# A source histogram kept in four quarters, with one copy per group of four tiles

## What is computed

```python
edge_index = jnp.stack([src, dst])                    # dst is sorted, src is not
msgs = jnp.exp(-edge_weight)[:, None] * x[dst]
out0 = jax.ops.segment_sum(msgs, src, num_segments=N_NODES)
seg_sum = jax.ops.segment_sum(edge_attr_32, src, num_segments=N)
seg_max = jax.ops.segment_max(edge_attr_32, src, num_segments=N)
```

## Time and profile before

| | us |
|---|---|
| median of three runs | 11958.36 |
| the profiled execution, whole | 11906.45 |
| its span, first to last instruction | 11904.7 |
| stage of the sort, first to last block's first scatter | 501.62 to 3457.44 |

### The profile page before, as it was taken

One profiled execution on the slowest core, in us unless ns is written; L12 is line 12 of the kernel. 1 busy time (PEld: TensorE's weight loads), 2 busy tenths in 40 slices (PEclk: granted clock), 3 DMA queues, 4 the chain that ended last, 5 costly groups with the idle time before them and its releaser, 6 DMA issues.

```text
span 11904.7 us, 66247 instructions
## 1 busy us (share of the span) xinstructions
PE 2340.7 (20%) x13804; PEld 1990.9 (17%) x13804; DVE 4863.0 (41%) x18501; ACT 1149.7 (10%) x3976; POOL 7239.8 (61%) x6880
## 2 busy tenths in 40 slices
PE   8755555555530041000000010000000100000000
PEld 7644444444420031000000010000000100000000
DVE  9744444444459932222222122222222444444445
ACT  0133333333320010000000000000000000000000
POOL 1555555555530035777777657777776677777776
PEclk7755555555555555555555555555555555555555
DMA  5122221222137701111111111111111122222221
GB/s 207 33 51 53 53 53 51 53 53 53 51 115 272 256 28 43 46 48 46 47 46 48 36 45 47 46 46 48 46 47 39 36 56 56 58 57 56 56 56 42
DMA packets 541753, 768.49 MB, mean 65 GB/s; under 512 B 328431, under 2 KB 341656, under 8 KB 528648
## 3 DMA queue, kind: packets, MB, share of 16 engines
q1 hardware_dynamic: 321544, 509.40, 12.8%
q0 software_dynamic: 219904, 255.88, 10.1%
HBM read 352.00 MB, written 412.82 MB: 64 GB/s over the span
## 4 chain that ended last, share of the span: by engine, by line
DVE 26%; issue 22%; POOL 20%; another core or an unknown queue 15%; PE 13%; ACT 4%; DVEq 1%; DMA 1%; SPq 0%; POOLq 0%
POOL arena_a L579 18%; DVE arena_a L1265 9%; DVE arena_a L1391 5%; PE bank L751 4%; PE bank L744 3%; DVE arena_a L1092 2%; DVE arena_a L1087 2%; PE bank L732 2%; PE bank L708 2%; PE bank L826 1%; DVE arena_a L1352 1%; ACT arena_b L663 1%; DVE arena_b L939 1%; PE bank L730 1%
## 5 line engine op out<-in xcount | busy, mean ns | idle before, releaser
L579 POOL DMA_INDIRECT arena_a<-table_c,decay x3136 | 3332.3, 1063 | 1326.1 <-issue 1002.6
L529 POOL DMA_INDIRECT by_src<-arena_b,idx_blk x1568 | 1553.0, 990 | 1500.5 <-ACT arena_b L656 1022.1
L1265 DVE SCALAR_TENSOR_TENSOR arena_a<-arena_a,same_dst 128x64 f32<-128x64 f32 x3134 | 892.3, 285 | 3447.7 <-DVE arena_a L1265 2029.0
L579 POOL DMA_INDIRECT arena_a<-table_at,decay x1568 | 1669.5, 1065 | 562.7 <-issue 474.1
L775 PE MATMUL bank<-ident,chunk_end 128*64 128x128 f32 (+2 forms) x8 | 2.7, 443 | 6672.6 <-DVEq L858 6672.6
L775 PEld LDWEIGHTS bank<-ident,chunk_end 128*64 128x64 f32 (+2 forms) x8 | 1.4, 240 | 6673.1 <-DVEq L858 6673.1
L988 DVE SCALAR_TENSOR_TENSOR arena_b<-bank,src_f,before 128x128 bf16<-128x128 f32 x1568 | 542.7, 346 | 1336.8 <-remote 1127.1
L751 PE MATMUL bank<-arena_b 98*128 98x128 f32 x3136 | 1056.4, 437 | 0.0
L744 PE MATMUL bank<-arena_b 128*98 128x128 bf16 x1568 | 526.2, 336 | 1382.7 <-ACT arena_b L663 913.5
L751 PEld LDWEIGHTS bank<-arena_b 98*128 98x128 f32 x3136 | 782.5, 306 | 0.0
L1391 DVE SCALAR_TENSOR_TENSOR arena_a<-arena_a,same_dst 128x68 f32<-128x68 f32 x1568 | 454.9, 290 | 458.6 <-DVE arena_a L1391 320.4
(11 more groups left out here) (251 smaller groups left out, 5287.3 us busy)
## 6 DMA issues: line engine op xcount, KB each, us to landing
states_src<-arena_a SPq DMA_DIRECT2D x98, 1024.0 KB
states_c<-arena_a SPq DMA_DIRECT2D x196, 512.0 KB
hrows<-by_src SPq DMA_DIRECT2D x98, 776.0 KB, 6.1
states_at<-arena_a SPq DMA_DIRECT2D x98, 576.0 KB
x_at_start<-arena_a SPq DMA_DIRECT2D x7, 7168.0 KB, 49.3
arena_a<-x_at_start SPq DMA_DIRECT2D x98, 512.0 KB, 3.7
arena_a<-table_c,decay POOLq DMA_INDIRECT x3136
arena_b<-in_a SPq DMA_DIRECT2D x98, 256.0 KB
```

The source lines that it names most:

```text
L529: pool.indirect_dma_start(out=by_src, out_offset=AT(ap=idx_blk[r][:, k:k + 1], axis=0), in_=rows[r][:, k, :], in_offset=None)\
L579: pool.indirect_dma_start(out=gb[r][:, k * w:(k + 1) * w], out_offset=None, in_=table[g], in_offset=AT(ap=src_i[:, n * J + k:n * J + k + 1 ...
L1265: ins = v.scalar_tensor_tensor(out=st[h][:, k * D:(k + 1) * D], in0=old, scalar=same_dst[:, e:e + 1], in1=gb[r][:, k * D:(k + 1) * D], op0 ...
```

## The change

`hist` becomes four histograms side by side in the same PSUM bank, one for each column modulo four, 98 x 512 in all. Quarter q of a tile's node starts at `base` plus the counts of the quarters before q. Tiles of one group no longer depend on each other, so the four tiles of a group share one copy (98x512), are added one after another, and are counted one after another. The order on each engine changes with it:

- ScalarE, for each group g: copy of the histograms for g+1, copy of the turned one-hots of g+1, then the four scalings of group g-2 (LAG is now 2, in groups). Before: 16 copies a block, and one scaling after each.
- TensorE, for each group g: four adds, twelve matmuls that turn group g+1, four counts. `hist_added` is raised once a group and no longer once a tile.
- In the bounds of the source, the histogram is counted into the four quarters; VectorE copies 98x512, sums over the quarters, and computes three further starts (98x128 each).
- `base` and the quarters live in the part of `arena_a` that is used early.

```diff
-LAG = 6
+LAG = 2
...
-        hist = bank[0][0:HIGH, 0:LOW]
+        hist = [bank[0][0:HIGH, q * LOW:(q + 1) * LOW] for q in range(Q)]
+        hist4 = bank[0][0:HIGH, 0:Q * LOW]
...
+            def snapped(g):
+                act.wait_ge(s("hist_added"), g + 1)
+                act.activation(snap[g % 2], hist4, ACT.Copy).then_inc(s("snap_ready"), 1)
+
+            snapped(0)
             turned(0)
-            for t in range(L):
-
-                act.wait_ge(s("hist_added"), t + 1)
-                act.activation(snap[t % 2], hist, ACT.Copy).then_inc(s("snap_ready"), 1)
-                if t % Q == 2 and t // Q + 1 < L // Q:
-                    turned(t // Q + 1)
-                if t >= LAG:
-                    scaled(t - LAG)
+            for g in range(L // Q):
+
+                if g + 1 < L // Q:
+                    snapped(g + 1)
+                    turned(g + 1)
+                if g >= LAG:
+                    for t in range((g - LAG) * Q, (g - LAG + 1) * Q):
+                        scaled(t)
...
-            pe.matmul(hist, ident[0:HIGH, 0:HIGH], base[:, :], start=True, stop=True).then_inc(s("hist_added"), 1)
+            pe.matmul(hist4, ident[0:HIGH, 0:HIGH], base4[:, :], start=True, stop=True).then_inc(s("hist_added"), 1)
...
+            def add(g):
+
+                pe.wait_ge(s("snap_ready"), g + 1)
+                for t in range(g * Q, (g + 1) * Q):
+                    h, k = t // J % 2, t % J
+                    last = pe.matmul(hist[t % Q], one(oh_hi[h], k), one(oh_lo[h], k), start=False, stop=True,
+                                     skip_group_check=True)
+                last.then_inc(s("hist_added"), 1)
+
+            def turn_group_of(g):
+
+                if g * Q % J == 0:
+                    pe.wait_ge(s("tile_onehots"), g * Q // J + 1)
+                if g >= 2:
+                    pe.wait_ge(s("ranked"), g - 1)
+                for t in range(g * Q, (g + 1) * Q):
+                    turn(t)
+
+            def count(g):
+
+                pe.wait_ge(s("hi_t_ready"), g + 1)
+                if g >= 2:
+                    pe.wait_ge(s("selected"), (g - 1) * Q)
+                for t in range(g * Q, (g + 1) * Q):
+                    at = slice(t % Q * P, (t % Q + 1) * P)
+                    last = pe.matmul(p_cnt[g % 2][:, at], hi_t[g % 2][:, at], snap[g % 2][:, at], start=True, stop=True)
+                last.then_inc(s("counted"), 1)
+
+            turn_group_of(0)
+            for g in range(L // Q):
+                add(g)
+                if g + 1 < L // Q:
+                    turn_group_of(g + 1)
+                count(g)
...
+                    link(v.tensor_copy(hist4_sb[:, :], hist4))
+                    link(v.tensor_reduce(hist_sb[:, :], hist4_sb[:, :].rearrange("p (q l) -> p l q", q=Q), AX.X, ALU.add))
...
+            for q in range(1, Q):
+                link(v.tensor_tensor(base4[:, q * LOW:(q + 1) * LOW], base4[:, (q - 1) * LOW:q * LOW],
+                                     hist4_sb[:, (q - 1) * LOW:q * LOW], ALU.add))
```

More of the change, by code:

```diff
@@ L262, in program @@
         hi_t = [cut["hi_t"][0:HIGH, q * Q * P:(q + 1) * Q * P] for q in range(2)]
-        snap = [cut["snap"][0:HIGH, q * P:(q + 1) * P] for q in range(2)]
+        snap = [cut["snap"][0:HIGH, q * Q * P:(q + 1) * Q * P] for q in range(2)]
         early = carve(arena_a, [("zeros", J * D), ("ih", Q * HIGH // 2), ("il", Q * LOW // 2),
-                                ("xs0", J * D), ("xs1", J * D), ("xb0", J * D), ("xb1", J * D)])
+                                ("xs0", J * D), ("xs1", J * D), ("xb0", J * D), ("xb1", J * D), ("base4", Q * LOW), ("hist4", Q * LOW)])
+        base4, hist4_sb = early["base4"][0:HIGH, :], early["hist4"][0:HIGH, :]
+        base = base4[:, 0:LOW]
         zeros = early["zeros"]
@@ L391, in _ @@
                 sp.wait_ge(s("bounds_ready"), n + 1)
-                sp.dma_start(bound[o, "start"], base[:, :] if o == "src" else diag[0:HIGH, :])\
+                sp.dma_start(bound[o, "start"], base if o == "src" else diag[0:HIGH, :])\
                   .then_inc(s("bounds_out"), 16)
@@ L701, in _ @@
                     pe.wait_ge(s("hist_read"), 1)
-                pe.matmul(hist, zero_b[:, 0:HIGH], zero_b[:, 0:LOW], start=True, stop=False)
+                streams = 1 if o == "dst" else Q
+                counts_to, nothing = (hist[0], zero_b[:, 0:LOW]) if o == "dst" else (hist4, bf(zero_b[:, 0:LOW], Q))
+                pe.matmul(counts_to, zero_b[:, 0:HIGH], nothing, start=True, stop=False)
                 def body(i):
@@ L707, in body @@
                         for k in range(J):
-                            last = pe.matmul(hist, one(oh_hi[h], k), one(oh_lo[h], k), start=False, stop=False)
+                            last = pe.matmul(hist[k % streams], one(oh_hi[h], k), one(oh_lo[h], k), start=False, stop=False)
                         last.then_inc(s("onehots_used"), 1)
                 turns(pe, body)
-                pe.matmul(hist, zero_b[:, 0:HIGH], zero_b[:, 0:LOW], start=False, stop=True)\
-                  .then_inc(s("hist_ready"), 1)
+                pe.matmul(counts_to, zero_b[:, 0:HIGH], nothing, start=False, stop=True).then_inc(s("hist_ready"), 1)
                 pe.wait_ge(s("row_totals"), n + 1)
@@ L736, in turn @@
                     spread.then_inc(s("src_spread"), 1)
[L738 to L762, removed]
-                    turn(ahead + t % Q * 2 + 1)
@@ L953, in _ @@
                 link(v.tensor_scalar(ends_sb[:, :], ends_sb[:, :], offs_sb[:, 0:1], None, ALU.add))
[L954 to L955 removed]
+                starts = base if o == "src" else diag[0:HIGH, :]
+                link(v.tensor_tensor(starts, ends_sb[:, :], hist_sb[:, :], ALU.subtract))
                 tell("bounds_ready")
```

13 lines of the change are left out of this document (6 added, 7 removed).

## The result

The changed kernel takes 11611.72 us (median of 4 runs, 11598.85 to 11628.68). The kernel before takes 11953.87 us (4 runs, 11948.19 to 11964.56). The ratio is 0.9715, with a 95% interval of 0.9698 to 0.9731. The forecast was 11560 us, the range 11010 to 11900. The profiled execution took 11606.91 us, its span is 11605.1 us. As the experiments will show, this gain belongs to the kind of chip that these runs were made on: on another chip (9) both kernels are faster and the change is 0.3% slower, and two variants of it are 0.3% slower on a third (11).

The account below looks back on a forecast made before the run. Bound: the sort's closed round of GpSimd's scatters and late signals, 30.47 us a block. Falling to 26.3 over 97 blocks saves 404 us, the start adds 6: 11508 us profiled, 11560 us median with 51.9 carried over; range 11010 to 11900.

Parts of the forecast that it names:

- The closed round and its bound: In the sort, GpSimd scatters a block for 20.45 us, then idles 10.30 us until ScalarE has scaled the next block.
- The release at +22.9: Signals held up during a block's scatter are all let go 22.9 us after it began, 2.5 us after its end.
- ScalarE's work behind the release: In the sort: copy 0.60, turned copy 0.60, three scalings 1.02, then 1.15 us to the next scatter; 26.3 us a block.
- turned copy 9: ScalarE's copy of group 9's turned one-hots (a block's groups 0 to 3, the next's 4 to 7), expected before the release.
- the start: Before the sort: 2.5 us more in the bounds of the source, 3.5 us for the later first scatter; together +6 us.
- The law of 0.79 us a matmul: During a scatter, from 4.5 us in until the release, TensorE's signals come at 0.79 us for each matmul.
- TensorE's signals alone: In the sort, the delay lies between TensorE's matmul and whoever waits for it, up to 11 us; none the other way.
- Held matmuls: Rival: during scatters TensorE's matmuls themselves are held, so the release frees nothing; 29.6 us a block, 11880 us, chance 0.18.
- The place and not the time: Slower rival: the stall in the sort is tied to a tile's place; 35.2 us a block, some 12420 us, chance 0.14.
- Slow signals gone: Rival: the new order raises no slow signals in the sort, GpSimd bounds at 20.75 us a block; gone or cheaper 0.15.
- a slower case of 0.14: The chance given to a slower kernel, by a stall tied to a tile's place in the sort: some 12420 us.
- The Trainium skill's 26 ns a signal: TensorE's signal increments cost about 26 ns each; three fewer in 392 groups would save 31 us; not used in the sum.

Follow-up runs that it names:

- a_unpacked: Changed kernel with its one-hot instructions in eight pieces, each written in the scalar-tensor-tensor form, against the kernel before: 11576.41 us, ratio 0.9713.
- b_split: Kernel before, with its one-hot instructions cut into one piece per group of four tiles: 11865.9 us, ratio 0.9961.

## Why the prediction was right, and where not

*The closed round and its bound.* Right on the chips with late signals. The gain is all idle time of GpSimd between scatters, in the sort. Over the rest nothing but 17 us moved.

*The release at +22.9.* Right: 23.2 in the median. But it lies between 0.8 us before and 2.95 us behind the end of the block's last scatter, so it isn't tied to that end to better than about 4 us. In one block of 26.8 us, for instance, it comes 0.6 us behind the end, at 1668.45.

*ScalarE's work behind the release.* This is the term that was mis-sized. I had turned copy 9 arrive at +18 to +20, and so only copy, turned copy and four scalings left, 3.37 us. Turned copy 9 is the release itself. Two more steps, it and the scalings of group 6, run behind it: 4.26 us. 23.2 + 4.26 = 27.4 us, the usual block, instead of 26.3. The difference between 27.22 and 26.3 over 97 blocks is 89 us. That the median missed by only 52 has three more terms: what lies behind the sort took 17 us more; the start cost 8 us less (I had 6 us more, it was 1.6 us less); and I had carried over that the median lies 51.9 us above the profiled execution, where it lay 4.8 us above, 47 us less. 89 + 17 - 8 - 47 = 51 us. That the last two terms took off half of the error was luck.

*The law of 0.79 us a matmul.* It fell. From the adds (signal at +10.4 as forecast) to the turns there are ten matmuls, 7.9 us by the law, and the signal took 12.8 us. In the block that begins at 1536.87 the first turn wasn't late itself: TensorE's rows start it right after the adds.

```profile
1541.47 0.63 PE L750 MATMUL bank<-arena_b 128*98 128x128 bf16 x4
1542.40 0.30 PE L737 MATMUL bank<-ident_b,arena_b 128*98 128x128 bf16 x1 [0.30 <-DVE arena_b L1010]
```

The copy (L651) that needs these turns of 1542.40 starts at 1560.09, 17 us later. The law fitted one gap of one block in the trace before, and that gap could as well be one hand-off. I have no law in its place. A count of hand-offs, one late and the next at the release, describes both kernels and most blocks of three variants, but not `a_unpacked`, where two come late before the release, nor `b_split`, where 22 of 82 blocks show it.

*Not TensorE's signals alone.* I had put the delay between TensorE and whoever waits for it. VectorE's wait for its own `selected` ends late too, at the same moment as ScalarE's copy:

```profile
1547.28 0.29 DVE L1022 SCALAR_TENSOR_TENSOR arena_b<-bank,arena_b 128x128 bf16<-128x128 f32 x1 [1.55 <-remote]
```

*Some matmuls are late themselves.* I had put all of the delay behind TensorE's matmuls. In 90 of 91 blocks of the changed kernel at least one of the twelve matmuls that turn a group starts more than 0.5 us after the matmul before it, though no wait stands between them in the code. It is nearly always one of the last three:

```profile
1521.94 0.27 PE L737 MATMUL bank<-ident_b,arena_b 128*98 128x128 bf16 x1
1523.36 0.28 PE L739 MATMUL bank<-ident_b,hi_src 128*128 128x128 bf16 x1 [1.15 <-issue]
1525.47 0.27 PE L739 MATMUL bank<-ident_b,lo_src 128*128 128x128 bf16 x1 [1.83 <-issue]
```

The longest such step is 2.85 us. All fall inside a scatter or within 3 us behind it, and in the two traces of chip 9 there is none over 0.16 us. They cost this block nothing that the rows show, since the release comes 7 us later (8.4 us in the median).

*The rivals.* Held matmuls (29.6 us a block) has a true part, the one just told, but is out as what sets the block: at the release ScalarE passes three TensorE hand-offs without idle time, so these matmuls had been done. The place and not the time (35.2 us) is out: the stall comes at another place in each variant and at the same time. Slow signals gone (20.8 us a block, GpSimd never idle) is what the chips 9 and 11 show, but for the kernel before as well, so it brought no gain there. I had a slower case of 0.14 by a wrong mechanism; the slower case that exists, another chip where GpSimd is the bound, I didn't have. Nothing in one trace of one chip speaks for it, except that a signal being 11 us late is itself strange.

*The Trainium skill's 26 ns a signal* ("TensorE: Matmul & The Clock Gate", "The cost: per-tile semaphore tail"). No run here resolves it: twelve signals more a block gave 1.0031 on chip 11 where the changed kernel had 1.0032 on chip 9, and TensorE isn't the bound there.

## What to carry to other kernels

A round that is closed by one release pays for what stands behind it on one engine; but look at what the release will be after a change of order, for here the new order slid the same chain along in 66 of 91 blocks. Time both kernels on several chips before believing a gain that comes out of a wait which the profile calls "remote": here 342 us were gained on one and 32 us lost on another. Where GpSimd issues indirect DMAs back to back, try to cut VectorE's long two-operand instructions beside them into short pieces: it costs 0.4 us of VectorE a block and gave 0.4% in the kernel before, on a chip with late signals. Where GpSimd is the bound it wasn't tried.

## What was not expected of the hardware

- The same program takes 10200 us on chips 9 and 11 and 11918 to 11954 us on chips 7 and 8 and in the first runs. On the slower ones signals between engines, and an engine's to itself, come up to 17 us late while GpSimd's indirect DMAs run, and single matmuls that wait for nothing start up to 2.85 us after the one before. What makes them late, and why on some chips, stays open. That it needs the indirect DMAs wasn't tried on such a chip: the kernels without them ran on chip 11.
- A scatter of 0.96 us takes up to 2.01 us when it starts during an instruction of VectorE with two SBUF operands, packed or not, and can be held over several such instructions in a row.
- The sort's granted clock rose from 0.56 to 0.67 in the changed kernel, with TensorE busy 48% instead of 53%. No term of the sum hangs on it.
